# Order of the products and of VectorE's work in the last stage of a two-layer graph kernel

## The chip, the cores and the metric

The kernel runs on one core of one Trainium2 chip. The metric is the device time of one execution in microseconds (us). PE is TensorE (PEld its weight loads), DVE is VectorE, ACT is ScalarE, POOL is GpSimd, SP is SyncE, whose queue issues most transfers.

## The reference

Input are 64 graphs of 128 nodes with 256 features (`x`) and 64 adjacency matrices of 128 x 128 (`adj`). Three blocks follow each other. The first is a transformer layer: layer norm, attention with 8 heads over the nodes of a graph with the adjacency in the logits and in the weights, an output projection, and a feed-forward part with GELU. The second and third are graph attention layers over the block's output. For the change only the last one matters; for one graph, with `x` the result so far:

```
n   = layer_norm(x, g2, b2)
h   = n @ W2                              # 128 x 256, one head
s, t = h @ a_src2, h @ a_dst2             # one number per node
e   = leaky_relu(s[:, None] + t[None, :], 0.2) + adj
out = softmax(e, axis=-1) @ h + x
```

## The kernel before, in words

All graphs stay in SBUF (`x_all`). The kernel goes through four stages, one per layer norm: attention, feed-forward, first graph attention, second graph attention (`c2_step`, the last stage). Each stage works in 16 steps (`NC`), a step on a chunk of G = 4 graphs. Every engine has its own function `c2_step(i, half, par)`, written out by hand, and runs its instructions in that order; semaphores order the engines against each other. `par` is the parity of the step: the even chunks use PSUM banks 0 to 3, the odd ones 4 to 7, one bank per graph.

Matrix products whose precision matters are made of three products: an operand is split into a high part (`hi`, `xh`, rounded to the fast type fp32r) and a low part (`lo`, `xl`, the rest), and hi x hi, hi x lo and lo x hi are summed. With two halves of the contraction (KT = 2) that is six products for each graph.

What happens to chunk i in the last stage:

- ACT normalises the four graphs into `xn` (`normalise`, L1124) in step i - 1, with mean and deviation that the DVE took from `x_all` two and three steps ahead (`stats`, L309; `aggr`, L314) and POOL turned into factors (L961 to L970).
- PE transposes `xn` into two banks (`d_ln_turn`, L1579), at the end of its step i - 1. ACT copies them as high parts (`d_hi`, L1258), the DVE subtracts to get the two low parts (`d_lo`, kt 0 and 1, L736).
- In step i PE computes h and the two scores of each graph into the graph's bank (`d_h_of`: L1685 and L1686 with the high parts, two each, then L1689 with the low parts, two). ACT copies h to SBUF (`d_h_out`, L1262) and the score columns into `sd` (`d_columns`, L1266), once for the graphs 0 and 1 and once for 2 and 3. PE transposes the scores (`d_turn`, L1697), the DVE takes the maximum (`d_bias`, L706 and L708), and ACT makes three rows of exponentials (`d_exps`, L1273), one of which POOL limits (L942).
- In step i + 1 PE multiplies rows to outer products in the graph's bank (`d_outer`, L1709) and turns a row into columns (L1711), which ACT copies as `f_col` (`d_f_out`, L1278). The DVE makes the weights from them, the scaled copies (`d_scale`, L720, four graphs), and PE multiplies them with h, again in the graph's bank (`d_av`, L1715). The DVE divides by the sum and adds the residual (`d_norms`: a reciprocal L727 and `y`, L731): graph 0 and graph 1 in step i + 1, graphs 2 and 3 at the beginning of step i + 2. SP then sends the chunk out (L890).

So a step of the DVE works in this order: outputs of the graphs 2 and 3 of chunk i - 2, `aggr`, four `stats`, `d_scale` of chunk i - 1, `d_bias` of chunk i, output of graph 0 of chunk i - 1, both low parts of chunk i + 1, output of graph 1 of chunk i - 1. A step of PE: h of graph 0, h of graph 1, outer products of chunk i - 1, h of graphs 2 and 3, the first output product of chunk i - 1, turn of the scores, transposes of chunk i + 1, the other three output products.

A product that opens a bank waits until the DVE has read the chunk of two steps before from it (`wait_for(pe, d_y, (i - 2) * G + (g + 1))`); the outer products wait for the low parts of the next chunk, since its transposes lie in the same banks.

Of the kernel before, what the change touches and what calls it, by code (L numbers as in the profile page):

```python
# [28 lines left out]
P = 128  # L29
D = 256  # L30
KT = D // P
G = 4
# [15 lines left out]
def wait_for(eng, sem, value):  # L48

    if isinstance(value, int) and value <= 0:  # L50
        return
    eng.wait_ge(sem, value)


def build(nc, x, adj, wq, bq, wk, bk, wv, bv, wo, bo, g1, b1, g2, b2, wf1, bf1, wf2, bf2,
# [7 lines left out]
    with ctx:  # L63
# [15 lines left out]
        whl, at_wf1 = {}, 0  # L79
# [118 lines left out]
        CA, CB, CC, CD = 0, NC, 2 * NC, 3 * NC  # L198
        BK = ctx.enter_context(nc.psum_tensor("BK", [P, 8, 512], F32))
# [8 lines left out]
        def ln_bank(i, par, kt):  # L208

            return F[kt] if isinstance(i, int) and i == 1 else BK[:, 4 * (1 - par) + kt, :]  # L210
# [50 lines left out]
        def nm_count(c, first):  # L261

            return c if first == CA else c - (CC - NC)

        def xs(i, g):
            return x_all[:, bass.ds((i * G + g) * D, D)]

        def gts(i, g):
            return gt_all[:, bass.ds((i * G + g) * P, P)]

        def chunks(eng, step, n=NC):

            for i in range(n):
                step(i, i // 2, i % 2)
# [32 lines left out]
        def _(dve):  # L307
            def stats(c, i, g):
                dve.bn_stats(st[:, g, :], xs(i, g)).then_inc(ln_st, 1)  # L309

            def aggr(c):

                for g in range(G):
                    dve.bn_aggr(mv[:, g, :], st[:, g, :]).then_inc(ln_mv, 1)  # L314
# [388 lines left out]
            def d_bias(i, par):  # L703

                dve.wait_ge(d_t, i + 1)
                dve.tensor_reduce(d_max[:], T_ps[par][:, P:2 * P], AX, ALU.max).then_inc(d_mx, 1)  # L706
                dve.wait_ge(d_mx, i + 1)
                dve.scalar_tensor_tensor(out=turn_bias[:], in0=turn_coef[:], scalar=d_max[:, 0:1], in1=turn_const[:],  # L708
                                         op0=ALU.mult, op1=ALU.add).then_inc(d_tb, 1)

            def d_cap(i):
                dve.wait_ge(d_ex, i * 3 + 1)
                dve.tensor_scalar(b_row[:], b_row[:], ROW_LIMIT, None, ALU.min).then_inc(d_cp, 1)

            def d_scale(i, par):
                dve.wait_ge(d_q, i + 1)
                dve.wait_ge(d_fc, i + 1)
                wait_for(dve, d_o, i * G)
                for g in range(G):
                    dve.scalar_tensor_tensor(out=pp[0][:, g, :], in0=BK[:, 4 * par + g, 0:P], scalar=f_col[:, g:g + 1], in1=gts(i, g),  # L720
                                             op0=ALU.max, op1=ALU.mult).then_inc(d_pp, 1)

            def d_norms(i, half, par, first, last):
                if first == 0:
                    dve.wait_ge(y_out[par], half * 16 + Y_START)
                dve.wait_ge(d_o, i * G + last + 1)
                dve.reciprocal(crec[:, first:last + 1, 0:1], BK[:, 4 * par + first:4 * par + last + 1, D:D + 1]).then_inc(d_rec, 1)  # L727
                dve.wait_ge(d_rec, i * 3 + min(first, 2) + 1)
                for g in range(first, last + 1):
                    dve.wait_ge(d_xb, i * G + g + 1)  # L730
                    dve.scalar_tensor_tensor(out=y_sb[par][:, g, :], in0=BK[:, 4 * par + g, 0:D], scalar=crec[:, g, 0:1],  # L731
                                             in1=xs(i, g), op0=ALU.mult, op1=ALU.add).then_inc(d_y, 1)

            def d_lo(i, par, kt):
                dve.wait_ge(ln_xh, (i + CD) * KT + kt + 1)
                dve.tensor_tensor(xld[par][:, kt, :], ln_bank(i, par, kt), xhd[par][:, kt, :].bitcast(F32), ALU.subtract).then_inc(ln_xl, 1)  # L736
# [47 lines left out]
            def c2_step(i, half, par):  # L784
                at = i if isinstance(i, int) else 2
                back, old = at >= 1, at >= 2
                more, ahead, far = (not (isinstance(i, int) and i >= NC - n) for n in (1, 2, 3))
                older = (i - 2, half - 1, par)
                prev = (i - 1, half - (1 - par), 1 - par)
                if ahead:  # L790
                    dve.wait_ge(ln_nm, nm_count(i + CD + 1, CD))
                    dve.wait_ge(ln_st, (i + CD + 3) * G)
                if old:
                    d_norms(*older, 2, 3)
                if ahead:
                    aggr(i + CD + 2)
                if far:
                    dve.wait_ge(ln_mv, (i + CD + 3) * G)
                    for g in range(G):
                        stats(i + CD + 3, i + 3, g)  # L800
                if back:
                    d_scale(i - 1, 1 - par)
                d_bias(i, par)
                if back:
                    d_norms(*prev, 0, 0)
                if more and at >= 1:
                    d_lo(i + 1, 1 - par, 0)
                    d_lo(i + 1, 1 - par, 1)
                if i == 0:
                    d_cap(i)  # L810
                if back:
                    d_norms(*prev, 1, 1)
            chunks(dve, c2_step)
            d_cap(NC - 1)
            d_norms(NC - 2, NC // 2 - 1, 0, 2, 3)
# [521 lines left out]
        def _(pe):  # L1337
# [337 lines left out]
                c_av(NC - 1, last, h)  # L1675


            def d_h_of(i, par, g):

                hi, lo = whl["w2"]  # L1680
                dst, n = BK[:, 4 * par + g, 0:D + 2], slice(g * P, (g + 1) * P)
                pe.wait_ge(ln_xh, (i + CD) * KT + KT)
                wait_for(pe, d_y, (i - 2) * G + (g + 1))
                for kt in range(KT):
                    pe.matmul(dst, xhd[par][:, kt, n], hi[:, kt, :], start=(kt == 0), stop=False)  # L1685
                    pe.matmul(dst, xhd[par][:, kt, n], lo[:, kt, :], start=False, stop=False)  # L1686
                for kt in range(KT):
                    pe.wait_ge(ln_xl, (i + CD) * KT + kt + 1)
                    r = pe.matmul(dst, xld[par][:, kt, n], hi[:, kt, :], start=False, stop=(kt == KT - 1))  # L1689
                r.then_inc(d_h, 1)  # L1690

            def d_turn(i, par):

                pe.wait_ge(d_sd, i * 2 + 2)
                pe.wait_ge(d_hc, i * G + 3)
                for k in range(2):
                    r = pe.transpose(T_ps[par][:, k * P:(k + 1) * P], sd[:, k, :], ident[:])  # L1697
                r.then_inc(d_t, 1)

            def d_outer(i, par):  # L1700

                pe.wait_ge(d_cp, i + 1)
                pe.wait_ge(d_ex, i * 3 + 3)
                pe.wait_ge(d_hc, i * G + G)
                if not (isinstance(i, int) and i == NC - 1):
                    pe.wait_ge(ln_xl, (i + CD + 1) * KT + KT)
                for g in range(G):
                    row = slice(g * 32, g * 32 + 1)
                    r = pe.matmul(BK[:, 4 * par + g, 0:P], e_row[row, :], b_row[row, :], start=True, stop=True, tile_position=(g * 32, 0))  # L1709
                r.then_inc(d_q, 1)  # L1710
                pe.matmul(FC_ps[par], f_row[:], ident[:, 0:P:32], start=True, stop=True).then_inc(d_ft, 1)  # L1711

            def d_av(i, par, g):
                pe.wait_ge(d_pp, i * G + g + 1)
                pe.matmul(BK[:, 4 * par + g, 0:D + 1], pp[0][:, g, :], hc[par][:, g, :], start=True, stop=True).then_inc(d_o, 1)  # L1715

            def c2_step(i, half, par):
                back = not (isinstance(i, int) and i == 0)
                more = back and not (isinstance(i, int) and i == NC - 1)
                d_h_of(i, par, 0)  # L1720
                d_h_of(i, par, 1)
                if back:
                    d_outer(i - 1, 1 - par)
                d_h_of(i, par, 2)
                d_h_of(i, par, 3)
                if back:
                    d_av(i - 1, 1 - par, 0)
                d_turn(i, par)
                if more:
                    d_ln_turn(i + 1, 1 - par, 0)  # L1730
                    d_ln_turn(i + 1, 1 - par, 1)
                if back:
                    for g in range(1, G):
                        d_av(i - 1, 1 - par, g)
# [33 lines left out]
```

## Time and profile before

| | us |
|---|---|
| median of 3 runs | 1100.36 (1098.8 to 1100.59) |
| the profiled execution | 1107.71 |
| its span | 1105.9 |
| PE busy (matmul) | 1051.9, 95% |
| DVE busy | 799.6, 72% |
| ACT busy | 714.2, 65% |
| POOL busy | 405.4, 37% |

The span goes from the first to the last instruction of the profiled execution. Shares are means over stages that work differently. The last stage runs from about 980 us to the end; its steps 2 to 15 begin with products at 996.94 and 1089.08. The rows below give start times on the span's clock, so that a distance is a difference of two starts; a duration runs to the end of an instruction's last write and can overlap the next instruction on the same engine.

### The profile page before, as it was taken

Reading aid. Unit: us, or ns where it says so; the run is one execution under the profiler, and the core shown is the slowest. Engines: PE = TensorE matmul, PEld = TensorE weight load, DVE = VectorE, ACT = ScalarE, POOL = GpSimd, SP = SyncE. Lnnn points to the kernel's source line nnn. Section 1 sums busy time; section 2 is a strip of 40 time slices with the busy share of each in tenths; the row PEclk is TensorE's granted clock in tenths of the full one; section 3 lists DMA queues with packets and bytes.
Section 4 is the critical chain, followed back from the end, with each engine's and each line's share of the span. In section 5 each row is a group of like instructions: output and inputs, shape, how many; then the busy total and the mean of one; then the engine's idle time right before and its main releaser. Section 6 shows DMA issues by size and latency. Waiting matters only on the chain.

```text
span 1105.9 us, 39179 instructions
## 1 busy us (share of the span) xinstructions
PE 1051.9 (95%) x15924; PEld 921.6 (83%) x15924; DVE 799.6 (72%) x1921; ACT 714.2 (65%) x1718; POOL 405.4 (37%) x642
## 2 busy tenths in 40 slices
PE   5999999999999989999999999999899999969997
PEld 5888888888888868899989988998788888868886
DVE  4577777777777668856565656545778988949986
ACT  2777677777677745554455455446668888847774
POOL 3531121121121103421132113112368888876673
PEclk9999999999999999999999999999879999989999
DMA  9221111211110001110110011010000000002122
GB/s 241 50 46 41 41 41 41 74 45 41 41 41 12 12 14 50 30 26 20 28 31 20 21 29 29 20 39 11 19 14 28 19 19 28 4 2 78 67 72 94
DMA packets 82477, 43.67 MB, mean 39 GB/s; under 512 B 42913, under 2 KB 77985, under 8 KB 82337
## 3 DMA queue, kind: packets, MB, share of 16 engines
q1 hardware_dynamic: 78016, 41.44, 13.8%
q8 instruction: 98, 1.61, 0.6%
q10 hardware_dynamic: 4320, 0.28, 0.3%
q14 instruction: 43, 0.34, 0.1%
HBM read 21.25 MB, written 12.58 MB: 31 GB/s over the span
## 4 chain that ended last, share of the span: by engine, by line
PE 80%; DVE 8%; issue 4%; POOL 3%; ACT 2%; SPq 1%; DMA 1%; DVEq 0%; POOLq 0%; ACTq 0%
PE BK L1340 8%; PE BK L1342 8%; PE BK L1341 8%; PE BK L1469 6%; PE BK L1443 5%; PE BK L1556 5%; PE BK L1558 5%; PE BK L1557 5%; PE BK L1455 4%; PE BK L1436 3%; PE BK L1356 3%; PE BK L1365 3%; PE BK L1603 3%; PE BK L1357 2%; PE BK L1358 2%
## 5 line engine op out<-in xcount | busy, mean ns | idle before, releaser
L1188 ACT ACTIVATE gf<-BK,bcol 128x512 f32<-128x512 f32 x128 | 88.1, 689 | 159.9 <-PE BK L1342 146.3
L961 POOL TENSOR_TENSOR ve<-mv,eps_l 128x4 f32<-128x4 f32 x64 | 18.0, 281 | 441.2 <-DVE mv L314 419.8
L1104 ACT ACTIVATE e_sb<-BK,nmx 128x128 f32<-128x128 f32 x512 | 142.1, 408 | 28.5 <-DVE nmx L501 28.5
L597 DVE TENSOR_TENSOR gl<-gf,gh 128x512 fp32r<-128x512 f32 x128 | 100.8, 790 | 68.4 <-ACT gh L1189 66.3
L1556 PE MATMUL BK<-wf_hi,gh 128*128 128x256 f32 x512 | 142.7, 279 | 1.8 <-DVE gl L597 1.8
L1557 PE MATMUL BK<-wf_hi,gl 128*128 128x256 f32 x512 | 141.8, 277 | 0.0
L1558 PE MATMUL BK<-wf_lo,gh 128*128 128x256 f32 x512 | 141.7, 277 | 0.0
L507 DVE TENSOR_TENSOR pt_sb<-BK,ft 128x512 f32<-128x512 f32 x128 | 85.2, 686 | 59.4 <-PE BK L1443 57.9
L1124 ACT ACTIVATE xn<-x_all,neg_mr,rstd 128x256 f32<-128x256 f32 (+1 forms) x188 | 103.8, 611 | 4.7 <-POOL neg_mr L970 4.4
L1340 PE MATMUL BK<-xh,wf_hi 128*128 128x512 f32 x256 | 100.0, 390 | 1.3 <-DVE xl L341 0.8
L1342 PE MATMUL BK<-xh,wf_lo 128*128 128x512 f32 x256 | 100.9, 394 | 0.0
L1341 PE MATMUL BK<-xl,wf_hi 128*128 128x512 f32 x256 | 100.6, 393 | 0.0
L501 DVE TENSOR_REDUCE nmx<-BK 128x8 f32<-128x1024 f32 x64 | 76.7, 1219 | 30.9 <-PE BK L1436 30.9
L1556 PEld LDWEIGHTS BK<-wf_hi,gh 128*128 128x128 f32 x512 | 96.2, 188 | 3.3 <-DVE gl L597 2.6
L1557 PEld LDWEIGHTS BK<-wf_hi,gl 128*128 128x128 f32 x512 | 96.3, 188 | 0.7
L1558 PEld LDWEIGHTS BK<-wf_lo,gh 128*128 128x128 f32 x512 | 96.2, 188 | 0.0
L695 DVE SCALAR_TENSOR_TENSOR pp<-BK,gt_all 128x512 f32<-128x512 f32 x128 | 81.9, 682 | 19.0 <-PE BK L1603 19.0
L309 DVE BATCH_NORM_STATS2 st<-x_all 128x6 f32<-128x256 f32 (+1 forms) x256 | 90.7, 410 | 5.3 <-DMA x_all<-in_x_dram 4.8
L938 POOL TENSOR_TENSOR x_all<-x_all,bo_bc 128x256 f32<-128x256 f32 x64 | 44.6, 730 | 130.9 <-ACT xn L1124 118.6
L938 POOL TENSOR_TENSOR x_all<-x_all,c_bc 128x256 f32<-128x256 f32 (+1 forms) x128 | 90.7, 737 | 3.5 <-ACT xn L1124 1.8
L1189 ACT ACTIVATE gh<-BK,bcol 128x512 fp32r<-128x512 f32 x128 | 87.0, 680 | 0.0
L1443 PE MATMUL BK<-ident,e_sb 128*128 128x128 f32 x512 | 73.0, 275 | 1.2 <-ACT e_sb L1104 1.0
(207 smaller groups left out, 2785.7 us busy)
## 6 DMA issues: line engine op xcount, KB each, us to landing
x_all<-in_x_dram SPq DMA_DIRECT2D x16, 512.0 KB, 4.7
out_dram<-y SPq DMA_DIRECT2D x16, 512.0 KB, 2.9
xn<-tb_ln SPq DMA_DIRECT2D x240, 32.0 KB, 1.9
adj_in<-in_adj_dram SPq DMA_DIRECT2D x64, 64.0 KB, 3.6
adj_kept<-adj_tr SPq DMA_DIRECT2D x16, 256.0 KB, 2.3
adj_in<-adj_kept SPq DMA_DIRECT2D x16, 256.0 KB, 2.6
s_wf<-in_L_gnn_Wf_dram SPq DMA_DIRECT2D x2, 1024.0 KB, 6.8
s_w<-in_L_gnn_W_dram SPq DMA_DIRECT2D x2, 256.0 KB, 2.9
```

The source lines that it names most:

```text
L309: dve.bn_stats(st[:, g, :], xs(i, g)).then_inc(ln_st, 1)
L597: dve.tensor_tensor(gl[:, f, :], gf[f % 2][:], gh[:, f, :].bitcast(F32), ALU.subtract).then_inc(b_gl, 1)
L938: pool.tensor_tensor(xs(i, g), xs(i, g), bias[:], ALU.add).then_inc(signal, 1)
L1104: e = act.activation(e_sb[:, j, :], LE[:, r, q, :], ACT.Exp, bias=nmx[:, j:j + 1], scale=1.0)
L1124: act.activation(xn[:, g, :], xs(nxt, g), ACT.Identity, scale=rstd[:, g:g + 1], bias=neg_mr[:, g:g + 1]).then_inc(ln_xn, 1)
L1340: pe.matmul(dst, w_hi, m_hi, start=start, stop=False)
L1341: pe.matmul(dst, w_hi, m_lo, start=False, stop=False)
L1342: return pe.matmul(dst, w_lo, m_hi, start=False, stop=stop)
L1443: m = pe.transpose(LE[:, r, q, :], e_sb[:, 4 * r + q, :], ident[:])
L1556: pe.matmul(dst, gh[:, f, n], hi[:, f, :], start=(f == 0), stop=False)
L1557: pe.matmul(dst, gl[:, f, n], hi[:, f, :], start=False, stop=False)
L1558: r = pe.matmul(dst, gh[:, f, n], lo[:, f, :], start=False, stop=(f == FT - 1))
```

## The change

Three orders are changed in the last stage; the instructions, their sizes and their number stay the same. On PE the six products of a graph are divided into the four with high parts of x and the two with low parts, and two graphs are done as a pair: high of the first, high of the second, low of the first, low of the second. On the DVE the second low part moves behind the output of graph 1, and of the four `stats` two stay before `d_scale` and two go behind it.

```diff
@@ DVE, c2_step @@
                 if far:
                     dve.wait_ge(ln_mv, (i + CD + 3) * G)
-                    for g in range(G):
-                        stats(i + CD + 3, i + 3, g)
+                    stats(i + CD + 3, i + 3, 0)
+                    stats(i + CD + 3, i + 3, 1)
                 if back:
                     d_scale(i - 1, 1 - par)
+                if far:
+                    stats(i + CD + 3, i + 3, 2)
+                    stats(i + CD + 3, i + 3, 3)
                 d_bias(i, par)
                 if back:
                     d_norms(*prev, 0, 0)
                 if more and at >= 1:
                     d_lo(i + 1, 1 - par, 0)
-                    d_lo(i + 1, 1 - par, 1)
                 if i == 0:
                     d_cap(i)
                 if back:
                     d_norms(*prev, 1, 1)
+                if more and at >= 1:
+                    d_lo(i + 1, 1 - par, 1)
@@ PE @@
-            def d_h_of(i, par, g):
+            def d_h_hi(i, par, g):
...
                 for kt in range(KT):
                     pe.matmul(dst, xhd[par][:, kt, n], hi[:, kt, :], start=(kt == 0), stop=False)
                     pe.matmul(dst, xhd[par][:, kt, n], lo[:, kt, :], start=False, stop=False)
+
+            def d_h_lo(i, par, g):
+
+                hi = whl["w2"][0]
+                dst, n = BK[:, 4 * par + g, 0:D + 2], slice(g * P, (g + 1) * P)
                 for kt in range(KT):
                     pe.wait_ge(ln_xl, (i + CD) * KT + kt + 1)
                     r = pe.matmul(dst, xld[par][:, kt, n], hi[:, kt, :], start=False, stop=(kt == KT - 1))
                 r.then_inc(d_h, 1)
+
+            def d_h_pair(i, par, g):
+                d_h_hi(i, par, g)
+                d_h_hi(i, par, g + 1)
+                d_h_lo(i, par, g)
+                d_h_lo(i, par, g + 1)
...
-                d_h_of(i, par, 0)
-                d_h_of(i, par, 1)
+                d_h_pair(i, par, 0)
                 if back:
                     d_outer(i - 1, 1 - par)
-                d_h_of(i, par, 2)
-                d_h_of(i, par, 3)
+                d_h_pair(i, par, 2)
```

## Rows read from the trace of the kernel before

**Rows 1.** Busy time by stretch, steps 2 to 14: length, engines (instructions), PE clock, DMA.

```profile
996.94:1089.08 92.14, 89.32 (x678) 78.36 (x677) 81.58 (x288) 72.01 (x209) 63.03 (x113) 1.00 0.22 76
```

**Rows 2.** List of waits, 996.9 to 1096 us: total, times, longest.

```profile
DVE d_max L706 <- PE BK L1697: 7.1, 14, 0.9
...
PEld BK L1685 <- issue: 5.6, 14, 0.4
...
PE BK L1685 <- DVE y L731: 3.0, 13, 0.2
```

**Rows 3.** Timeline of PE, one step: start, duration, instruction, idle time before it.

```profile
1047.16 0.40 PE L1689 MATMUL BK<-w_hi,xl 128*128 128x258 f32 x2
1047.79 0.36 PE L1685 MATMUL BK<-w_hi,xh 128*128 128x258 f32 x1 [0.23 <-DVE y L731]
...
1048.23 0.28 PE L1686 MATMUL BK<-w_lo,xh 128*128 128x258 f32 x1
1048.35 0.40 PE L1689 MATMUL BK<-w_hi,xl 128*128 128x258 f32 x2
1048.68 0.50 PE L1709 MATMUL BK<-b_row,e_row 1*128 1x128 f32 x8
...
1050.88 0.60 PE L1715 MATMUL BK<-hc,pp 128*128 128x257 f32 x2
1051.31 0.44 PE L1697 MATMUL BK<-ident,sd 128*128 128x128 f32 x2
...
1052.46 1.47 PE L1715 MATMUL BK<-hc,pp 128*128 128x257 f32 x6
```

**Rows 4.** Timeline of the DVE, the same step.

```profile
1048.95 1.40 DVE L309 BATCH_NORM_STATS2 st<-x_all 128x6 f32<-128x256 f32 x4
1050.27 1.11 DVE L720 SCALAR_TENSOR_TENSOR pp<-BK,f_col,gt_all 128x128 f32<-128x128 f32 x4
1051.79 0.29 DVE L706 TENSOR_REDUCE d_max<-BK 128x1 f32<-128x128 f32 x1 [0.41 <-PE BK L1697]
...
1052.45 0.48 DVE L731 SCALAR_TENSOR_TENSOR y<-BK,crec,x_all 128x256 f32<-128x256 f32 x1
1052.85 1.29 DVE L736 TENSOR_TENSOR xl<-BK,xh 128x512 fp32r<-128x512 f32 x2
1054.06 0.16 DVE L727 RECIPROCAL crec<-BK 128x1 f32<-128x1 f32 x1
1054.25 0.48 DVE L731 SCALAR_TENSOR_TENSOR y<-BK,crec,x_all 128x256 f32<-128x256 f32 x1
```

**Rows 5.** Chain that ended last, end of the step: start, time in it, instruction.

```profile
1053.46 0.68 DVE xl L736
...
1054.88 0.36 PE BK L1685
```

**Rows 6.** Timeline of PE, outer products of steps 2 and 15.

```profile
998.96 0.50 PE L1709 MATMUL BK<-b_row,e_row 1*128 1x128 f32 x8
...
1091.28 0.50 PE L1709 MATMUL BK<-b_row,e_row 1*128 1x128 f32 x8
```

**Rows 7.** Timeline of ACT, the step of rows 3.

```profile
1046.85 1.11 ACT L1124 ACTIVATE xn<-x_all,neg_mr,rstd 128x256 f32<-128x256 f32 x2
1047.83 0.40 ACT L1262 ACTIVATE hc<-BK 128x256 f32<-128x256 f32 x1
...
1048.79 0.39 ACT L1262 ACTIVATE hc<-BK 128x256 f32<-128x256 f32 x1
1049.07 0.17 ACT L1266 ACTIVATE sd<-BK 128x4 f32<-128x4 f32 x1
1049.54 0.17 ACT L1278 ACTIVATE f_col<-BK 128x4 f32<-128x4 f32 x1 [0.30 <-PE BK L1711]
...
1050.36 0.39 ACT L1262 ACTIVATE hc<-BK 128x256 f32<-128x256 f32 x1
1051.08 0.18 ACT L1266 ACTIVATE sd<-BK 128x4 f32<-128x4 f32 x1 [0.33 <-PE BK L1689]
```

## The prediction

> **What bounds the kernel now.** The page comes first: its second part shows TensorE at nine tenths or more in nearly every slice, so I ask of the last stage alone what it waits for. The table by stretch has 92.14 us of it at a granted clock of 1.00 (2.4 GHz), PE busy for 89.32 [rows 1]: no clock is to be won there. The list of waits says where the rest is. The weight loads of L1685 stand idle 14 times for 5.6 us in all, up to 0.41 each; 13 times the product behind them is put down to the DVE's y (L731). The DVE in turn stands idle 14 times before d_max, for the turn on PE (L1697) [rows 2]. Two engines wait for each other in a ring, so it is the length of the ring and no engine's busy share that sets the time. The timelines of one step give it.
>
> Followed from the first high product of graph 1 to the same product one step later [rows 3 to 5]: L1685 at 1047.79, its low pair at 1048.35 (0.56), the outer products at 1048.68 (0.33), the first output product at 1050.88 (2.20, graphs 2 and 3 lie in it), the turn at 1051.31 (0.43), d_max at 1051.79 (0.48), y of graph 0 at 1052.45 (0.66), low part 0 at 1052.85 (0.40), the reciprocal of graph 1 at 1054.06 (1.21, both low parts), y of graph 1 at 1054.25 (0.19), L1685 of graph 1 at 1054.88 (0.63). Sum 7.09 us. The outer products of steps 2 and 15 start at 998.96 and 1091.28 [rows 6], 92.32 us for 13 steps: 7.10 each. The ring is the whole period. It closes because graph 1 writes a bank that holds the output of an earlier chunk until y of graph 1 has read it, and the DVE makes two low parts ahead of that y.
>
> **The change, part by part.**
>
> *Low part 1 behind y of graph 1.* Low part 1 starts at 1053.46 [rows 5], the reciprocal follows it at 1054.06 [rows 4]: 0.60 us leave the ring. Nothing else is passed there: d_cap sits between them only in step 0, which has no low part. The reciprocal then wants to run at 1053.46 and needs the output product of graph 1. The three of graphs 1 to 3 start at 1052.46; one takes 0.60 (1050.88) [rows 3], so it is there at 1053.06, 0.40 early. Behind low part 1 waits PE: the low products of graph 0, then of graph 1, then the outer products.
>
> *High products of two graphs first.* No product is added or dropped. What changes is what stands between the start of graph 1 and the outer products: it was four high and two low products, now it is four high, two low of graph 0 and two low of graph 1. Products of one kind follow each other in 0.12 (a pair lasts 0.40 at 1048.35, one of them 0.28), so 0.24 enter the ring.
>
> Is low part 1 there in time? It starts 0.40 after y of graph 1 (the step from y to low part at 1052.45 and 1052.85 [rows 4]) and takes 0.68 [rows 5], so it ends 1.08 after y starts. Graph 1 starts on PE 0.63 after y, so the low part ends at 0.45 on PE's count and, with about 0.12 for the signal (y ends at 1054.73, PE follows at 1054.88), is seen at 0.57 to 0.60. PE reaches the first low product at 0.56, which needs only low part 0, and the one that needs low part 1 at 0.68. Covered, by about 0.1. With the cover gone, each further 0.1 us costs 1.3 us over the stage.
>
> *Statistics split around the scaled copies.* Four statistics take 1.32 of the DVE's queue (1048.95 to 1050.27) [rows 4], so 0.66 move from before the copies to behind them. In before the copies start 3.12 after y of graph 1 (1050.27, less 1054.25 taken back by one period of 7.10). With low part 1 in between that would be 3.72; with the split it is 3.06, which is 2.43 after graph 1's start on PE. The first copy lasts under 0.4 and is done at 2.8; the output product asks for it at 0.56 + 0.24 + 0.33 + 2.20 = 3.33. Without the split it would be done at 3.5, 0.15 late. So the split keeps the gain of the other edits and I give it none of its own. What it risks is d_max, which has two statistics in front of it now. The DVE stands idle 0.41 of 7.10 there [rows 2, 4], so its queue alone needs 6.69, below the ring that follows, and d_max still waits for the turn by 0.08.
>
> *ACT, by the later end of graph 0.* In before its copy of graph 0 started 0.04 after graph 1 began (1047.83) [rows 7]. Now graph 0 ends with its low pair: 0.56 + 0.40 after graph 1's start, the copy at 1.0. Then come a normalisation of at most 0.49 (two and the copy's wait lie between 1046.85 and 1047.83), the copy of graph 1 at 1.0 + 0.28 + 0.49 = 1.77, the columns 0.28 later (1048.79 to 1049.07) and f_col, for which ACT is ready at about 2.12. The outer products are at 1.13 and f_col can follow them by 0.86 (1048.68 to 1049.54), at 1.99. So f_col ends at 2.29, and with 0.05 for the signal the copies at 2.43 don't wait. In the second pair graph 2 ends later by four high products, 0.48, so its copy moves from 1050.36 to 1050.84 and the last columns behind it to 1051.12 instead of 1051.08 [rows 7]. The turn waits for these: 0.04 (between 0 and 0.28, a whole copy; nearest to the row).
>
> *The ring after:* 7.10 - 0.60 + 0.24 + 0.04 = 6.78, a gain of 0.32 per step. What is late next is TensorE itself: with nothing to wait for it needs 7.10 less its idle 0.41 [rows 2], 6.69; or 7.10 less 0.47, 6.63, taken from the start of graph 1 (low pair of graph 0 at 1047.16, 0.24 for its two products, so 1047.40 instead of 1047.79, and 0.08 in a slow first product) [rows 3].
>
> *Sum.* 13 periods [rows 6] x 0.32 = 4.2. Step 2 gains a part of one more, between 0 and 0.32: I take 0.2. Steps 0 and 1 wait for a chain of normalisations on ACT and POOL, and the tail behind 1091.28 has no low part of a next chunk: nothing. SP's output transfer waits for y of graph 3, and its buffer is wanted again two steps later: nothing. Total 4.4 us. The profiled execution took 1107.71 (span 1105.9, 1.81 around it), 7.35 above the median of 1100.36; the steps that gain ran at a clock of 1.00, so the same 4.4 us are taken from the median: 1096.0.
>
> A rule that speaks against this. The y of graph 0 lasts from 1052.45 to 1052.93 while the low part starts at 1052.85 [rows 4]: DVE instructions overlap. The Trainium skill, in "VectorE: DVE Perf Modes", section "The DRAIN you can't avoid", says that the next operation does not start until the pipe of the one before is empty. By it no overlap could be counted on between the new neighbours, which is the second rival; the trace does not agree with it.
>
> **Rivals.**
>
> *TensorE without stalls.* If y of graph 1 comes a little sooner than counted, PE runs through, at 6.63 to 6.69 per step: 13 x 0.41 to 0.47 and 0.3 in step 2, 5.6 to 6.4 us, about 1094.4. For it: the ring's 6.78 lies within 0.15 of it. Against: f_col, low part 1 and the columns have 0.1 or less to spare each.
>
> *The DVE becomes the bound.* It has 0.41 idle per step and would use all but 0.09. Overlap with the next instruction is worth 0.08 a time (statistics last 1.40 and the copies follow after 1.32, y 0.48 and 0.40, low parts 1.29 and 1.21) [rows 4]. The edit makes three to five new neighbours (reciprocal behind low part 0, low part behind y, reciprocal behind low part 1, statistics behind copies, d_max behind statistics). Without overlap there, 6.69 + 0.24 to 0.40 = 6.93 to 7.09; in the middle 7.0, a gain of 13 x 0.1 + 0.2 = 1.5: 1098.9. Against: three of the five kinds overlap in the present order.
>
> *f_col late: slower than before.* Copies that start late now push two statistics in front of d_max. The place is ACT's queue from the copy of graph 0 to f_col. In before that took 1.71 (1047.83 to 1049.54) [rows 7]. If it stays so long and the copy of graph 0 starts only with the end of the pair, 1.24 after graph 1's start, f_col ends at 1.24 + 1.71 + 0.17 = 3.12 and the copies start at 3.17 instead of 2.43. Less d_max's 0.08 that lengthens the ring by 0.66 to 7.44: 13 x 0.34 - 0.2 = 4.2 slower, 1104.6. It decides from f_col ending at 2.46; from 2.78 on the whole gain is gone. For it: ACT works in order and gets graphs 0 and 1 nearly together. Against: much of the 1.71 was waiting, for graph 1 and the outer products.
>
> **How the numbers follow.** My own case (1095.0 to 1097.0, likeliest 1096.0) 0.62; TensorE without stalls 0.15; the DVE as bound 0.16; f_col late 0.07. About 0.2%, 2.2 us, is what a measurement of this kernel can tell from no change. Faster by more: the first two and the fast end of the third, 0.79; within it: the rest of the third, 0.14; slower 0.07. The range takes in the first rival and the middle of the second: 1093.8 to 1099.2.
>
> **What would show it.** Right: outer products (L1709) 6.7 to 6.8 us apart in the middle steps; the idle time before the first high product of graph 1 down from 0.41 to 0.1 or less, and none before the low products; d_max's idle time near 0.1; f_col ended when the first copy starts. Wrong: a stall of PE before the low products, which would mean that low part 1 is late; a DVE without idle time at a period near 7.0; copies that wait for f_col, or a turn that waits for the columns by more than 0.1. Then the gain is under 3 us.

## The result, and the profile after

The changed kernel takes 1096.88 us in the median of 20 runs (1093.51 to 1101.12), the kernel before 1102.1 us in 20 runs beside them (1098.77 to 1107.86). The ratio is 0.9949, 95% interval 0.9934 to 0.9963: 5.6 us faster, between 4.1 and 7.3. Forecast were 4.4 us and 1096.0.

Single runs of either kernel differ by up to 0.8%, and in the profiles TensorE's granted clock falls below 1.00 in a few stretches, not equally far in each run. So the measure for the experiments is the distance of the outer products (L1709 in before) from step 2 to step 15, all at a granted clock of 1.00, beside the ratio of times. Line numbers move by a few from kernel to kernel: L1709 of before is L1724 in the changed kernel, L1685 is L1689.

The table by stretch of the changed kernel: steps 2 to 14, then the stage's start, then from the outer products of step 15 to the end (length, busy PE, PEld, DVE, ACT, POOL, clock, DMA).

```profile
992.10:1080.18 88.08, 88.08 (x679) 78.23 (x677) 81.69 (x287) 68.57 (x207) 62.25 (x113) 1.00 0.23 79
974.48:992.10 17.62, 12.16 (x78) 10.90 (x79) 8.66 (x31) 7.67 (x26) 15.69 (x27) 0.81 0.00 0
1082.01:1095.20 13.19, 7.23 (x51) 5.55 (x50) 7.50 (x26) 2.55 (x11) 0.15 (x1) 0.95 0.35 121
```

92.14 us of [rows 1] have become 88.08, and PE shows no idle time in them, where it had 2.82. The end is 1.43 us shorter than in the profile of before (14.62 from 1091.28 to 1105.9), but there the clock was 0.85 and here 0.95; the start is 0.55 longer at a lower clock (0.81 against 0.90). With the clocks apart, neither can be put down to the change.

The outer products of steps 2 and 15 in the timeline of PE, the answer to [rows 6]:

```profile
993.83 0.50 PE L1724 MATMUL BK<-b_row,e_row 1*128 1x128 f32 x8
...
1082.01 0.50 PE L1724 MATMUL BK<-b_row,e_row 1*128 1x128 f32 x8
```

88.18 us for 13 steps, 6.78 each instead of 7.10: 4.1 us gained in the steps. One of them on PE, to be laid beside [rows 3]:

```profile
1039.47 0.47 PE L1689 MATMUL BK<-w_hi,xh 128*128 128x258 f32 x1
...
1040.18 0.36 PE L1689 MATMUL BK<-w_hi,xh 128*128 128x258 f32 x1
...
1040.62 0.28 PE L1690 MATMUL BK<-w_lo,xh 128*128 128x258 f32 x1
1040.74 0.64 PE L1698 MATMUL BK<-w_hi,xl 128*128 128x258 f32 x4
1041.31 0.50 PE L1724 MATMUL BK<-b_row,e_row 1*128 1x128 f32 x8
...
1043.51 0.60 PE L1730 MATMUL BK<-hc,pp 128*128 128x257 f32 x2
1044.00 0.41 PE L1712 MATMUL BK<-ident,sd 128*128 128x128 f32 x2
```

Graph 1 starts 0.71 after graph 0, four products further; the pause of 0.39 is gone. The four low products follow the last high one at the usual 0.12: low part 1 is in time. From graph 1's start to the outer products it is 1.13, as summed, and the turn comes 0.49 after the first output product, 0.06 later than in before. The same step on the DVE, beside [rows 4], and the addition on POOL that follows:

```profile
1038.75 0.69 DVE L736 TENSOR_TENSOR xl<-BK,xh 128x512 fp32r<-128x512 f32 x1
1039.36 0.16 DVE L727 RECIPROCAL crec<-BK 128x1 f32<-128x1 f32 x1
1039.55 0.48 DVE L731 SCALAR_TENSOR_TENSOR y<-BK,crec,x_all 128x256 f32<-128x256 f32 x1
1039.95 0.68 DVE L736 TENSOR_TENSOR xl<-BK,xh 128x512 fp32r<-128x512 f32 x1
...
1042.62 1.11 DVE L720 SCALAR_TENSOR_TENSOR pp<-BK,f_col,gt_all 128x128 f32<-128x128 f32 x4
1043.64 0.74 DVE L309 BATCH_NORM_STATS2 st<-x_all 128x6 f32<-128x256 f32 x2
1044.45 0.29 DVE L706 TENSOR_REDUCE d_max<-BK 128x1 f32<-128x128 f32 x1
1044.78 0.22 DVE L708 SCALAR_TENSOR_TENSOR turn_bias<-turn_coef,d_max,turn_const 128x3 f32<-128x3 f32 x1
...
1044.96 1.41 POOL L942 TENSOR_TENSOR x_all<-x_all,c_bc 128x256 f32<-128x256 f32 x2
```

The new neighbours overlap like the old ones (y to low part 0.40, low part to reciprocal 0.61), and the 0.41 of idle time before d_max are filled with two statistics. On ACT, beside [rows 7]:

```profile
1041.18 0.38 ACT L1266 ACTIVATE hc<-BK 128x256 f32<-128x256 f32 x1 [0.23 <-PE BK L1698]
...
1042.27 0.18 ACT L1282 ACTIVATE f_col<-BK 128x4 f32<-128x4 f32 x1
...
1043.47 0.38 ACT L1266 ACTIVATE hc<-BK 128x256 f32<-128x256 f32 x1 [0.53 <-PE BK L1698]
1043.75 0.17 ACT L1270 ACTIVATE sd<-BK 128x4 f32<-128x4 f32 x1
```

The copy of graph 0 starts 1.00 after graph 1. f_col ends at 1042.45 and the scaled copies start at 1042.62: hidden by 0.17. The waits, beside [rows 2], no longer hold the idle time of the first high products, nor y:

```profile
PEld BK L1712 <- ACT sd L1270: 3.8, 14, 0.3
...
DVE d_max L706 <- PE BK L1712: 2.5, 3, 0.9
```

The first row is the weight load of the turn, which waits for the score columns; before had 3.3 us there. The three waits left for d_max are the last steps, which have no statistics.

### The profile page after: what moved, and what is told of

Same layout as the page of the kernel before. It is cut to its first block, busy times and chain, and to the rows that moved or that the text cites. A ratio compares the mean times of both kernels' runs of the same rounds, so it can differ in the third digit from the quotient of the medians.

```text
span 1095.2 us, 39179 instructions
## 1 busy us (share of the span) xinstructions
PE 1043.2 (95%) x15924; PEld 915.1 (84%) x15924; DVE 799.9 (73%) x1921; ACT 710.2 (65%) x1718; POOL 405.0 (37%) x642
## 4 chain that ended last, share of the span: by engine, by line
PE 83%; DVE 5%; issue 4%; POOL 3%; ACT 2%; SPq 1%; DMA 1%; POOLq 0%; DVEq 0%; ACTq 0%
PE BK L1344 8%; PE BK L1346 8%; PE BK L1345 8%; PE BK L1473 6%; PE BK L1447 5%; PE BK L1560 5%; PE BK L1561 5%; PE BK L1562 5%; PE BK L1459 4%; PE BK L1440 3%; PE BK L1360 3%; PE BK L1369 3%; PE BK L1607 3%; PE BK L1361 2%; PE BK L1362 2%
```

## The experiments

Theory: a step is as long as the ring that was summed up, so an edit counts by what it takes from the ring or puts in. Rival: each edit helps by itself, the pairs by covering waits or the DVE's order by releasing y sooner. All kernels are given by their difference to before or to the changed kernel. The results first: the mean step from 2 to 15, 13 steps against before, and the ratio of times to the kernel before on the same chip.

| kernel | step, us | 13 steps, us | ratio (95%) |
|---|---|---|---|
| before | 7.10 | | |
| changed | 6.78 | -4.1 | 0.9949 (0.9934 to 0.9963) |
| pairs alone | 7.37 | +3.5 | 1.0040 (1.0016 to 1.0065) |
| low part alone | 7.15 | +0.7 | 1.0014 (0.9995 to 1.0032) |
| split alone | 7.10 | 0.0 | 0.9995 (0.9973 to 1.0017) |
| pairs and split | 7.37 | +3.5 | 1.0029 (1.0007 to 1.0052) |
| low part and split | 7.15 | +0.7 | 1.0006 (0.9985 to 1.0027) |
| pairs and low part | 7.23 | +1.7 | 1.0013 (0.9995 to 1.0032) |
| the same, additions wait | 6.89 | -2.7 | 0.9976 (0.9959 to 0.9994) |
| all four statistics behind | 7.38 | +3.6 | 1.0044 (1.0024 to 1.0063) |
| the same, additions wait | 7.24 | +1.7 | 1.0011 (0.9989 to 1.0033) |
| changed, pair for 0 and 1 only | 6.74 | -4.7 | 0.9948 (0.9926 to 0.9969) |
| changed, one more addition | 6.98 | -1.6 | 1.0002 (0.9983 to 1.0022) |
| changed, one more fill | 6.79 | -4.1 | 0.9959 (0.9943 to 0.9975) |

### Pairs alone, and pairs with the split

The DVE's part of the change is undone, or its split alone kept:

```diff
                 if more and at >= 1:
                     d_lo(i + 1, 1 - par, 0)
+                    d_lo(i + 1, 1 - par, 1)
...
                     d_norms(*prev, 1, 1)
-                if more and at >= 1:
-                    d_lo(i + 1, 1 - par, 1)
```

> Only the products in pairs; both low parts stay ahead of y of graph 1, statistics together. Ring theory: the ring still holds both low parts (nothing leaves it) and gains the low pair of graph 0 (0.24) and the columns' 0.06, so a step takes 7.10 + 0.30 = 7.40 us and the kernel is 13 x 0.30 = 3.9 us slower than before. Rival (the pairs are the gain by themselves, since eight high products cover the waits for the DVE): a step takes 6.8 and the kernel is 4 us faster.

> Pairs and split, both low parts ahead of y of graph 1. Ring theory: as with the pairs alone, 7.40 a step, 3.9 us slower than before; the split adds nothing to it. Rival (pairs need only that the copies come in time): 6.8.

Both 7.37. PE in the kernel with the pairs alone:

```profile
1036.77 0.47 PE L1685 MATMUL BK<-w_hi,xh 128*128 128x258 f32 x1
...
1038.07 0.36 PE L1685 MATMUL BK<-w_hi,xh 128*128 128x258 f32 x1 [0.47 <-DVE y L731]
```

Graph 1 still starts 1.30 after graph 0, as in before, and now two low products more stand between it and the outer products. The pairs make the kernel slower by themselves; the rival falls.

### Low part alone, and with the split

```diff
-                    d_lo(i + 1, 1 - par, 1)
...
                     d_norms(*prev, 1, 1)
+                if more and at >= 1:
+                    d_lo(i + 1, 1 - par, 1)
```

> Only low part 1 moved behind y of graph 1; PE computes graph 0 whole, then graph 1, as before. Ring theory: y of graph 1 comes 0.60 sooner, but now low part 1 is seen by PE 1.08 + 0.12 us after y starts, graph 0's last product waits for it, and graph 1 starts 0.12 behind that: 1.32 after y instead of 0.63. A step takes 7.10 - 0.60 + 0.69 = 7.19, the kernel is 1 us slower or the same. Rival (the sooner y is the gain by itself): a step takes 6.5 to 6.7, 5 us faster.

> Low part moved and split, PE's order as before. Ring theory: as with the low part alone, 7.19 a step, 1 us slower than before or the same. Rival (the DVE's order is the gain, PE's has no part in it): 6.7 to 6.8.

7.15 in both, 0.04 under the ring's sum. PE in the kernel with the low part alone:

```profile
1042.06 0.28 PE L1690 MATMUL BK<-w_hi,xl 128*128 128x258 f32 x1
1042.60 0.39 PE L1690 MATMUL BK<-w_hi,xl 128*128 128x258 f32 x1 [0.26 <-DVE xl L736]
1042.83 0.28 PE L1686 MATMUL BK<-w_hi,xh 128*128 128x258 f32 x1
```

The wait has moved from graph 1's first product to graph 0's last. The pairs exist to put graph 1's high products into that gap: either edit loses alone, and both together gain. For the low part alone only the steps show the loss; its time is not distinct from that of before.

### The split alone

```diff
-                    for g in range(G):
-                        stats(i + CD + 3, i + 3, g)
+                    stats(i + CD + 3, i + 3, 0)
+                    stats(i + CD + 3, i + 3, 1)
...
+                if far:
+                    stats(i + CD + 3, i + 3, 2)
+                    stats(i + CD + 3, i + 3, 3)
```

> Only the statistics split around the scaled copies. Ring theory: neither the copies nor the statistics lie in the ring, d_max waits for the turn by 0.41 in before: a step takes 7.10, no change. Rival (an earlier copy frees the DVE for d_max): 6.9 or less.

7.10, as the ring has it.

### Pairs and low part, without the split

The changed kernel with the split taken back.

> Pairs and low part moved, the four statistics together ahead of the scaled copies. Ring theory: the copies start 0.66 later, the first output product follows a copy's start by 0.41 at the least and has 0.48 spare to lose from where it stands in the changed kernel's trace (1042.62 to 1043.51 less 0.41), so it is 0.18 late, of which the turn's wait for the columns hides 0.06: a step takes 6.77 + 0.12 = 6.89 and the kernel is 13 x 0.21 = 2.7 us faster than before. Rival (the split does nothing, the DVE's queue has the same work in any order): 6.77, 4.4 us faster. Rival (the split is most of the gain, because d_max had to wait): 7.0 or more.

This missed. The steps come in kinds: 7.47 in eight of them, 6.92 in two, 6.8 where there are no statistics or the stage begins. The timeline of three steps, DVE and POOL, shows what differs:

```profile
1007.65 0.78 DVE L708 SCALAR_TENSOR_TENSOR turn_bias<-turn_coef,d_max,turn_const 128x3 f32<-128x3 f32 x1
1007.69 1.41 POOL L939 TENSOR_TENSOR x_all<-x_all,c_bc 128x256 f32<-128x256 f32 x2
1008.36 0.15 DVE L727 RECIPROCAL crec<-BK 128x1 f32<-128x1 f32 x1
...
1022.59 0.22 DVE L708 SCALAR_TENSOR_TENSOR turn_bias<-turn_coef,d_max,turn_const 128x3 f32<-128x3 f32 x1
1022.64 1.46 POOL L939 TENSOR_TENSOR x_all<-x_all,c_bc 128x256 f32<-128x256 f32 x2
...
1029.52 0.22 DVE L708 SCALAR_TENSOR_TENSOR turn_bias<-turn_coef,d_max,turn_const 128x3 f32<-128x3 f32 x1
1029.66 1.42 POOL L939 TENSOR_TENSOR x_all<-x_all,c_bc 128x256 f32<-128x256 f32 x2 [0.18 <-POOL neg_mr L971]
```

turn_bias works on 128 x 3 numbers and lasts 0.22, but 0.78 when POOL's addition starts with it, and it then ends with the first of the two additions (1007.69 and some 0.73). No list of waits names it: it stands as busy time of the DVE and as "issue" in the chain. Both of turn_bias's tensors and both of the addition's lie in SBUF. In the two short steps the DVE came first, by a recorded 0.05 at 1022.59 and by 0.14 at 1029.52. POOL's pause of 0.18 in the second is no effect of the meeting: the same step of before and of the changed kernel has it too, with turn_bias at 0.22. Four kernels below test this.

### The additions wait for turn_bias

In POOL's order, on the kernel without the split and on the one with all four statistics behind the copies:

```diff
                     if first == CD:
+                        if i > 0:
+                            pool.wait_ge(d_tb, i)
                         add_bias(i, CD, c2_bc, d_xb)
```

> Pairs and low part moved, statistics together, and POOL's additions to x_all (L939) wait until the DVE has made turn_bias (L708). In the run without this wait turn_bias lasted 0.78 us in the steps of 7.47 and 0.22 in those of 6.92, and the long ones ended with the first addition on POOL. Theory of the shared operand path (turn_bias, whose two tensors both lie in SBUF, is held up while POOL's addition of two SBUF tensors runs): turn_bias lasts 0.22 in all steps, a step takes 6.9 us as the ring has it, and the kernel is 13 x 0.2 = 2.6 us faster than before. Rival (the long steps come from something else, such as the late copies): steps of 7.47 stay.

```profile
1047.27 0.20 POOL L971 TENSOR_TENSOR neg_mr<-zero_g,ve 128x4 f32<-128x4 f32 x1
...
1047.51 0.22 DVE L708 SCALAR_TENSOR_TENSOR turn_bias<-turn_coef,d_max,turn_const 128x3 f32<-128x3 f32 x1
...
1047.87 1.42 POOL L939 TENSOR_TENSOR x_all<-x_all,c_bc 128x256 f32<-128x256 f32 x2 [0.39 <-POOL neg_mr L971]
```

All steps with statistics are at 6.91 to 6.94 now, turn_bias at 0.22; 6.89 in the mean. A wait added on POOL made the kernel faster, from +1.7 us to -2.7 against before.

### All four statistics behind the copies

```diff
                 if far:
                     dve.wait_ge(ln_mv, (i + CD + 3) * G)
-                    stats(i + CD + 3, i + 3, 0)
-                    stats(i + CD + 3, i + 3, 1)
                 if back:
                     d_scale(i - 1, 1 - par)
                 if far:
+                    stats(i + CD + 3, i + 3, 0)
+                    stats(i + CD + 3, i + 3, 1)
                     stats(i + CD + 3, i + 3, 2)
                     stats(i + CD + 3, i + 3, 3)
```

> The changed kernel with all four statistics behind the scaled copies. Ring theory: the copies can start 0.66 sooner on the DVE but f_col (ends at 1042.45 in the changed kernel's trace, copies at 1042.62) lets them start only 0.12 sooner; four statistics then stand ahead of d_max, and a step takes 7.2 us: slower than before by about 1 us. Rival (d_max waits for the turn anyway, so the place of the statistics costs nothing): 6.77.

> All four statistics behind the scaled copies, and POOL's additions wait for turn_bias. Theory of the shared path: turn_bias goes from 0.40 to 0.22 and 0.2 us leave each step, 7.47 to 7.27; still slower than before by 2 us, by the late d_max. Rival (the copies' wait for f_col is all of it): 7.47.

About 7.47 in the steps with statistics, 0.27 above the 7.2 that was expected, and 7.29 once the additions wait. The first kernel's timeline:

```profile
1011.45 0.18 ACT L1281 ACTIVATE f_col<-BK 128x4 f32<-128x4 f32 x1
1011.83 1.13 DVE L720 SCALAR_TENSOR_TENSOR pp<-BK,f_col,gt_all 128x128 f32<-128x128 f32 x4 [0.74 <-ACT f_col L1281]
1012.87 1.39 DVE L309 BATCH_NORM_STATS2 st<-x_all 128x6 f32<-128x256 f32 x4
1014.15 1.41 POOL L941 TENSOR_TENSOR x_all<-x_all,c_bc 128x256 f32<-128x256 f32 x2
1014.18 0.27 DVE L706 TENSOR_REDUCE d_max<-BK 128x1 f32<-128x128 f32 x1
1014.49 0.40 DVE L708 SCALAR_TENSOR_TENSOR turn_bias<-turn_coef,d_max,turn_const 128x3 f32<-128x3 f32 x1
```

The DVE stands idle 0.74 for f_col, then four statistics stand before d_max: what the prediction's third rival feared, made to happen. Here f_col is not late (it ends 1.13 after the outer products, as in the changed kernel); the DVE comes to the copies sooner. 0.51 of the step (6.78 to 7.29) are the price of the late d_max, and 0.18 are turn_bias beside POOL, which the expected 7.2 had not counted. Here turn_bias lasted 0.40: the addition that held it had been running since 1014.15.

### An addition, or a fill, put under turn_bias

On the changed kernel, behind `rstd_of` in POOL's last stage; one run with the first line, one with the second:

```diff
                             rstd_of(i + CD + 2, EPS[CD])
+                            pool.tensor_tensor(spare[:, 0:340], spare[:, 340:680], spare[:, 680:1020], ALU.add)
+                            pool.memset(atc[:], 0.0)
```

> The changed kernel with one more addition on POOL in each step, of two SBUF tensors of 340 columns in a buffer that nobody reads any more, placed behind rstd (L967): from 1044.41 to about 1045.4 in the step whose turn_bias starts at 1044.78. Theory of the shared path: turn_bias lasts until that addition ends, the reciprocal behind it starts 0.4 us later, and a step takes 7.2 us instead of 6.78. Rival (turn_bias does not depend on POOL; only the later factors could matter, which have 1.5 us to spare): 6.78.

> The same place and about the same duration (0.95 us), but POOL only fills the buffer with zeros and reads nothing. Theory of the shared path: it is the reading of SBUF that collides, turn_bias lasts 0.22 and a step takes 6.78. Rival (any work of POOL at that place holds the DVE up, or the delay of the factors by 0.95 us costs): 7.2 as with the addition.

The timeline with the addition:

```profile
1043.98 0.91 POOL L995 TENSOR_TENSOR atc<-atc 128x340 f32<-128x340 f32 x1
1044.44 0.46 DVE L708 SCALAR_TENSOR_TENSOR turn_bias<-turn_coef,d_max,turn_const 128x3 f32<-128x3 f32 x1
1044.83 0.15 DVE L727 RECIPROCAL crec<-BK 128x1 f32<-128x1 f32 x1
```

And with the fill:

```profile
1044.26 0.95 POOL L994 MEMSET atc<- 128x1024 f32 x1
...
1044.74 0.22 DVE L708 SCALAR_TENSOR_TENSOR turn_bias<-turn_coef,d_max,turn_const 128x3 f32<-128x3 f32 x1
```

turn_bias ends at 1044.90 with the addition (1044.89), 0.24 late, and a step takes 6.98. I had counted 0.4, with an addition that starts later and lasts 0.1 longer than it did. The fill, as long and at the same place, leaves 0.22 and 6.79. So it is POOL's addition, which reads SBUF, that holds turn_bias up, and neither POOL's work as such nor the later factors.

### A pair only where it is needed

```diff
-                d_h_pair(i, par, 2)
+                for g in (2, 3):
+                    d_h_hi(i, par, g)
+                    d_h_lo(i, par, g)
```

> The changed kernel with the pair only for graphs 0 and 1; graphs 2 and 3 are each computed whole, as before. Ring theory: graph 2's copy on ACT comes early again, the columns of graphs 2 and 3 follow the last product at once and the turn starts 0.43 after the first output product instead of 0.49: a step takes 6.71, 0.7 us faster than the changed kernel, which a time can't show but the distance of the outer products can. Rival (DVE's queue of 6.69 to 6.77 is what binds now): no change, 6.77.

```profile
1041.42 0.59 PE L1730 MATMUL BK<-hc,pp 128*128 128x257 f32 x2
1041.85 0.43 PE L1712 MATMUL BK<-ident,sd 128*128 128x128 f32 x2
```

The turn is back at 0.43 and a step takes 6.74, so the DVE's queue was not the bound at 6.78. Its ratio to before, 0.9948, is not distinct from that of the changed kernel; in the steps it is 0.6 us better, the best of all kernels here.

## Why the prediction was right

The time lies 0.9 us from the forecast and the difference 1.2 us above the forecast's, inside the range either way. That the time comes so near is partly luck: the forecast started from 1100.36, the median of three runs, and the kernel before took 1102.1 in the 20 runs beside the changed one. This 1.7 and the larger difference offset each other. The steps of the prediction:

- *Low part 1 out of the ring, a low pair into it.* Right in size. The step was put at 6.78 and is 6.78. That the 7.09 added up to the period proves no ring: start distances do so along any way back to the same instruction. What shows it are the waits that close it (y before L1685, the turn before d_max) and the edits alone. The same sum gave 7.40 for the pairs alone (with the turn's 0.06 as measured in the changed kernel) and 7.19 for the low part alone before they ran, and they took 7.37 and 7.15. That two edits lose alone and gain together follows from the ring and contradicts the rival by which each helps by itself.
- *The columns of graphs 2 and 3.* 0.04 were counted, the turn came 0.06 later. The kernel with one pair gives 0.04 of it back.
- *f_col and low part 1 in time.* Right; f_col was ready 0.17 before the copies, counted were 0.14.
- *TensorE next.* Open. PE shows no idle time in steps 2 to 14 at 6.78 a step, yet the kernel with one pair does the same products in 6.74. So a PE that shows as busy throughout still holds short waits, and no kernel here came to the floor of 6.63 to 6.69.
- *The split.* Right that it has no gain of its own (7.10 alone) and keeps the others'. Without it the prediction had the first output product 0.15 late. So it is: with POOL's additions held back the ten steps of 6.91 to 6.94 lie 0.15 above 6.78 (0.11 in the mean of all 13). But a later turn_bias also meets POOL's addition, which costs another 0.55 in eight of the 13 steps (7.47 against 6.92), and with it the whole gain. This collision stands in no part of the prediction. In before, turn_bias started 0.12 ahead of the addition, and in the changed kernel 0.18 (1044.78 and 1044.96 above). The step of before:

```profile
1052.12 0.22 DVE L708 SCALAR_TENSOR_TENSOR turn_bias<-turn_coef,d_max,turn_const 128x3 f32<-128x3 f32 x1
...
1052.24 1.41 POOL L938 TENSOR_TENSOR x_all<-x_all,c_bc 128x256 f32<-128x256 f32 x2
```

  So the forecast held with a margin that it had not looked at, and that was luck. The trace of before already has the collision in step 1 of the stage, where the addition starts 0.04 ahead and turn_bias lasts 0.70:

```profile
994.69 1.41 POOL L938 TENSOR_TENSOR x_all<-x_all,c_bc 128x256 f32<-128x256 f32 x2
994.73 0.70 DVE L708 SCALAR_TENSOR_TENSOR turn_bias<-turn_coef,d_max,turn_const 128x3 f32<-128x3 f32 x1
```

- *Step 2's 0.2 us.* Open: the start of the stage ran at a clock of 0.81 against 0.90, which hides it.
- *5.6 us in the times against 4.1 in the steps.* 4.1 is the interval's near end. The rest is not explained by the steps and stays open. The kernel with the fill, with the same steps, has 0.9959, 4.5 us; the one with one more addition gains 1.6 us in the steps and nothing in the time (1.0002). So a time here can lie about 2 us beside its steps.

The rule of the Trainium skill that was weighed against the change ("VectorE: DVE Perf Modes", "The DRAIN you can't avoid") would have had the new neighbours not overlap; they did, by 0.08. The same section adds that a next operation that is not held starts earlier, which the prediction left out and which the overlap agrees with.

## What to carry to other kernels

Where two engines wait for each other, write down the ring with its distances and the waits that close it, and judge every edit by what it moves into or out of it: two edits can lose alone and gain together, and a wait's idle time is not the gain. An instruction of a few numbers in such a ring is worth a look for what its operands share with another engine. A wait that is added where nothing is late can make a kernel faster.

## What the runs showed of the hardware

turn_bias, a DVE instruction with two tensors in SBUF, is held up while POOL runs an addition that reads SBUF: it took 0.78 instead of 0.22 when a 128 x 256 addition of 0.73 started with it, 0.46 under a 128 x 340 addition of 0.91, and 0.22 under a fill of 0.95 that only writes. The profile shows it as a longer duration, not as a wait. y, which reads one of its two tensors from PSUM, keeps its 0.48 beside the same additions (1052.45 in [rows 4], the addition from 1052.24). A small subtraction on POOL (neg_mr, 128 x 4, 0.20) shows no such effect: in the kernel with one pair it starts 0.04 ahead of turn_bias at 1042.65, which lasts 0.22.

The Trainium skill says this in "SBUF — State Buffer", section "Who interferes with whom": a DVE instruction with two SBUF inputs contends with a GpSimd instruction that reads SBUF, not with one that only writes. It adds that the order of issue decides who blocks. The runs agree, with the starts as recorded: additions that began 0.34 and 0.46 ahead of turn_bias held it to their end, and a turn_bias 0.05 or more ahead of the additions to x_all kept 0.22 in every step of every kernel here. One that was 0.02 to 0.04 ahead was still held, in eight steps of the kernel without the split; why the line lies there and not at zero is open.
